# The last four attention tiles in a written-out order, and where a weight transpose stands in the SyncE queue (cross-attention and quantized feed-forward, one core)

## The chip, the cores and the metric

One Trainium2 chip, one core, one launch of the whole program. The time is the device time of that launch in microseconds. Three runs of the kernel before give a median of 570.4 us (570.27 to 570.66).

## What is computed

Eight sequences of 512 rows of 512 numbers, each with its own context of 77 rows of 384. A layer norm, cross-attention with 8 heads of 64, an output product with a bias and a residual; then a second layer norm and a gated feed-forward of width 1408 whose activations and weights are fake-quantized, the activations by a scale over the whole tensor, and a second residual.

```python
def xattn(x, context):                      # x already normed
    q, k, v = heads(x @ Wq), heads(context @ Wk), heads(context @ Wv)
    a = softmax(einsum('bhsd,bhld->bhsl', q, k) * 64 ** -0.5)
    return merge(einsum('bhsl,bhld->bhsd', a, v)) @ Wo + bo
x = x + xattn(layernorm(x), ctx)
xq = act_quant(layernorm(x), clip_x)        # scale: max |.| of all 8*512*512 numbers / 127
h = silu(xq @ w_quant(w_gate).T) * (xq @ w_quant(w_up).T)
x = x + act_quant(h, clip_down) @ w_quant(w_down).T
```

## The kernel before, in words

The 4096 rows are 32 row tiles of 128; a batch b is the four tiles 4b to 4b+3. The order on every engine is written out by hand: each helper appends one instruction (or one group) to the list of its engine with the tokens (semaphore, value) that it waits for, and each engine runs its list in order. A DMA is issued by SyncE ("SPq"), in the order of its list as well; both transposing DMAs are in that list (L39).

`attend(s)` (L647), called for s = 0 to 31 (L844), is one step of a software pipeline. For tile s it turns the normed probabilities (`PT`, L425: five transposes into the bank pair `PTP`; `PT_high` on ScalarE and `PT_low` on VectorE split them into a high and a low half in `pts`). For tile s+1 it makes the scores (`S`, L375, into the bank pair `SP`), takes the maximum and subtracts it (`soft_max`, `soft_sub`, VectorE), exponentiates (ScalarE), sums and inverts (VectorE) and multiplies by the inverse (`soft_norm`, GpSimd). `S(n)` waits for `soft_sub(n-1)`, since both use `SP`. For tile s-5 it makes the output product (`wo`, L487: 12 matmuls into the single bank `WOP`), adds the residual (`residual`, L517, VectorE, whose result `x1` is stored) and the statistics of the second norm (`second_stats`, `second_aggr`, `second_scale`). For s-6 it norms (`normed`, L541, ScalarE; the result `n2` is stored to `n_rows` in HBM), for s-7 it takes the largest magnitude (`largest`, L548). Four buffers of `x1` and of `n2` exist (RR = 4): `normed(n)` waits for the landing of the store of `n2` of tile n-4.

At t = 0 of a batch the product with the values of the batch before is made (`PV_rest`, `PV`, L448 to L481) in the two banks of `QO` and the two of `SP`; its results are split into `os`, which `wo` reads. Up to s = 23 there are also projections of queries (`q_chunk`) into `QO`; from s = 24 on there are none, and `QO` is used by `PV` alone.

The weights of the feed-forward are quantized on the way (`w_load` to `w_integer`) and their integers stored. Two transposing DMAs bring them back: `wgu` (gate and up, L858) and `wd` (down, L926). The diagonal of the four scales of `w_down` rows (L854, VectorE) is spread to all partitions by four matmuls with ones into the bank `MI` (`spread_scale`, L834) and copied to `sdb`.

After the loop come `wo(27)`, `PV` of batch 7, and for the tiles 28 to 31 product, residual, statistics, norm and largest (L878). With that the barrier is reached: `whole_scale(0)` (L904) reduces the 32 columns of largest magnitudes to one number on all partitions, with small matmuls between (`keep_clock`, L896). The first four tiles of `n2` are loaded back into `n2b` (L887), multiplied by the scale (`quant_y`), rounded (`quant_top`, `quant_low`), turned (`turn`) and fed to the feed-forward's matmuls (`ffn`, L968). `quant_top` writes over memory of the first half, and so waits for `flown` (L925): the landing of all stores of `x1` and `n2` of the tiles 28 to 31.

The SyncE list around this place: the twelve loads of `vbd` for batch 7, then the transpose `wgu`, then stores of `x1` and `n2` as they come, four loads of `n2b` after the stores of tile 30's `x1`, the last stores, four more loads, the transpose `wd`.

## Time and profile before

| | |
|---|---|
| median of three runs | 570.4 us |
| the profiled execution | 570.46 us, span of its instructions 568.6 us |
| start to the last tiles (0 to 271.2 us) | TensorE busy 258.2 us |
| last tiles of attention (271.2 to 294.3) | TensorE busy 18.9 of 23.1 us, VectorE 21.35 |
| PV of batch 7 and the last four products (294.3 to 309.4) | TensorE busy 15.1 of 15.1 us |
| barrier (309.4 to 320.7) | TensorE busy 9.75 of 11.3 us |
| gate and up products (320.7 to 484.6) | TensorE busy 163.84 of 163.9 us |
| down products and the end (484.6 to 568.6) | TensorE busy 77.2 of 84.0 us |

The profiled execution's own time is 0.06 us above the median, and 1.9 us above its span. A row of the trace gives start, length, engine, line of the code, operation, and what it writes and reads; in brackets stands the idle time of the engine before it and who ended it. Starts are counted from the first instruction. Short operations of one engine overlap by some 0.1 us, so that lengths may add up to more than the time between starts.

### The profile page before, as it was taken

The numbers are of one execution on the slowest core, as the hardware profiler recorded it, in microseconds if no ns is written. First come the engines' busy times: TensorE is split into PE (matmuls) and PEld (weight loads), VectorE is DVE, ScalarE is ACT, GpSimd is POOL, SyncE is SP. The second block draws the span as 40 slices with busy tenths as digits, with TensorE's granted clock in tenths as the row PEclk, the third lists the DMA queues.
The fourth block names the chain that finished last, engine by engine and source line by source line (L and its number), as shares of the span: only waits on it lengthen the run. The fifth ranks groups of instructions, "written<-read, shape, count | busy, mean of one in ns | idle before, by whom it ended". The sixth has DMA issues, their size and how long they took to land.

```text
span 568.6 us, 8277 instructions
## 1 busy us (share of the span) xinstructions
PE 543.0 (95%) x2811; PEld 360.7 (63%) x2811; DVE 471.8 (83%) x874; ACT 310.4 (55%) x436; POOL 233.9 (41%) x352
## 2 busy tenths in 40 slices
PE   4999889999999999999899899999999999899997
PEld 2978678787888878787668544444444446443443
DVE  2747888989989888998987689889888988879883
ACT  3743546556464755544342666666666643999300
POOL 3576758679595968856342000000000000054442
PEclk9999999999999999999999999999999999999999
DMA  8708365756657573633295917541020010299887
GB/s 309 256 38 277 107 196 171 249 168 207 214 178 231 194 249 115 215 118 126 73 317 189 261 62 278 203 148 47 29 75 1 0 38 1 100 339 217 118 107 119
DMA packets 67779, 90.16 MB, mean 159 GB/s; under 512 B 32049, under 2 KB 34865, under 8 KB 67481
## 3 DMA queue, kind: packets, MB, share of 16 engines
q1 hardware_dynamic: 63413, 81.77, 44.6%
q0 software_dynamic: 4320, 7.87, 9.3%
q8 instruction: 22, 0.36, 0.3%
q14 instruction: 20, 0.16, 0.1%
q10 hardware_dynamic: 4, 0.00, 0.0%
HBM read 47.51 MB, written 37.78 MB: 150 GB/s over the span
## 4 chain that ended last, share of the span: by engine, by line
PE 50%; issue 34%; DVE 8%; DMA 5%; ACT 1%; POOL 1%; SPq 0%; POOLq 0%; DVEq 0%
PE QO L194 6%; PE QO L196 6%; PE QO L195 6%; PE SP L382 5%; PE WOP L495 4%; PE WOP L493 4%; PE WOP L494 4%; DMA out<-n2b 2%; PE PTP L1082 2%; PE PTP L430 2%; PE QO L1082 2%; PE SP L1082 2%; DMA wkr<-in_xattn_Wk 2%; PE MI L1082 1%; PE WOP L1082 1%
## 5 line engine op out<-in xcount | busy, mean ns | idle before, releaser
L45 POOL DMA_DIRECT2D out<-n2b x30 | 30.2, 1039 | 219.1 <-DVE n2b L1093 219.1
L977 PE MATMUL QO<-nT,wgu 128*128 128x512 bf16 x352 | 90.3, 379 | 0.6 <-ACT nT L221 0.6
L977 PE MATMUL SP<-nT,wgu 128*128 128x512 bf16 x352 | 90.3, 379 | 0.0
L983 ACT ACTIVATE sil<-QO,fsc 128x512 f32<-128x512 f32 x88 | 60.5, 687 | 50.7 <-PE QO L977 45.4
L987 DVE SCALAR_TENSOR_TENSOR h<-SP,fsc,sil 128x512 f32<-128x512 f32 x88 | 65.9, 749 | 14.9 <-PE SP L977 14.7
L422 POOL TENSOR_TENSOR PN<-P,rs 128x512 f32<-128x512 f32 x64 | 44.2, 712 | 57.8 <-DVE rs L414 57.8
L405 ACT ACTIVATE P<-P,r 128x616 f32<-128x616 f32 x32 | 26.0, 812 | 69.5 <-DVE P L401 69.5
L990 DVE TENSOR_REDUCE hmx<-h 128x1 f32<-128x512 f32 x88 | 60.4, 686 | 3.0
L977 PEld LDWEIGHTS SP<-nT,wgu 128*128 128x128 bf16 x352 | 34.4, 98 | 41.5
L977 PEld LDWEIGHTS QO<-nT,wgu 128*128 128x128 bf16 x352 | 33.2, 98 | 35.4 <-ACT nT L221 0.7
L194 PE MATMUL QO<-xTs,wqs 128*128 128x512 f32 x128 | 52.0, 407 | 1.8 <-DVE xTs L225 1.3
L196 PE MATMUL QO<-xTs,wqs 128*128 128x512 f32 x128 | 50.1, 391 | 0.0
L195 PE MATMUL QO<-xTs,wqs 128*128 128x512 f32 x128 | 49.9, 390 | 0.0
L1051 ACT ACTIVATE h<-h,magic,g 128x1536 f32<-128x1536 f32 (+2 forms) x38 | 47.8, 1354 | 3.7 <-DVE g L222 3.7
L493 PE MATMUL WOP<-wos,os 128*128 128x512 f32 x116 | 47.6, 411 | 0.2 <-DVE x L519 0.2
L495 PE MATMUL WOP<-wos,os 128*128 128x512 f32 x116 | 45.9, 395 | 0.0
L494 PE MATMUL WOP<-wos,os 128*128 128x512 f32 x116 | 45.8, 395 | 0.0
L382 PE MATMUL SP<-kst,qs 128*128 128x154 f32 x256 | 39.5, 296 | 5.0 <-DVE P L401 2.9
L514 POOL TENSOR_TENSOR xn<-xn,bob 128x512 f32<-128x512 f32 x32 | 41.2, 1291 | 0.0
L590 ACT ACTIVATE wraw<-wraw,magic,wiv 128x512 f32<-128x512 f32 (+1 forms) x26 | 24.1, 928 | 30.3 <-DVE wiv L583 30.3
L382 PEld LDWEIGHTS SP<-kst,qs 128*128 128x128 f32 x256 | 35.5, 190 | 7.3 <-DVE P L401 3.8
L543 ACT ACTIVATE n<-x,mr,r 128x512 f32<-128x512 f32 x32 | 25.8, 807 | 20.0 <-POOL mr L537 20.0
(169 smaller groups left out, 1162.9 us busy)
## 6 DMA issues: line engine op xcount, KB each, us to landing
xTr<-in_xT SPq DMA_DIRECT2D x8, 1024.0 KB, 8.0
xn<-in_x SPq DMA_DIRECT2D x32, 256.0 KB, 3.8
out<-x SPq DMA_DIRECT2D x32, 256.0 KB, 2.9
n_rows<-n SPq DMA_DIRECT2D x32, 256.0 KB, 2.6
n2b<-n_rows SPq DMA_DIRECT2D x32, 256.0 KB, 4.2
out<-n2b POOLq DMA_DIRECT2D x30, 256.0 KB, 4.4
h_spill<-h SPq DMA_DIRECT2D x2, 2816.0 KB, 9.3
h<-h_spill SPq DMA_DIRECT2D x6, 768.0 KB, 7.8
```

The costliest lines, as they stand in the source:

```text
L194: e.matmul(ps, lh, rh, start=(i == 0), stop=False)
L195: e.matmul(ps, lh, rl, start=False, stop=False)
L196: m = e.matmul(ps, ll, rh, start=False, stop=(i == n - 1))
L382: m = e.matmul(o, qs[:, b % 2, j, w], kst[:, b, j, :], start=(j % 2 == 0), stop=True, skip_group_check=True)
L493: e.matmul(wo_bank(n), os_[:, 0, j, w], wos[:, 0, j, :], start=(j == 0), stop=False)
L494: e.matmul(wo_bank(n), os_[:, 0, j, w], wos[:, 1, j, :], start=False, stop=False)
L495: return e.matmul(wo_bank(n), os_[:, 1, j, w], wos[:, 0, j, :], start=False, stop=(j == 3))
L977: m = e.matmul(ps, wv_[:, k, col:col + 128], nT[:, b % 2, k, :], start=(k == 0), stop=(k == 3))
L983: t_sil[n] = add("act", lambda e: e.activation(sil[:, n % SR, :], gp, ACT.Silu, scale=fsc[:, ic:ic + 1]), [t_g[n], t_fs, t_h.get(n - SR)] ...
L987: t_h[n] = add("dve", lambda e: e.scalar_tensor_tensor(out=hv, in0=up, scalar=fsc[:, 11 + ic:12 + ic], in1=sil[:, n % SR, :], op0=ALU.mult ...
L990: t_hm[n] = add("dve", lambda e: e.tensor_reduce(hmx[:, n:n + 1], hv, AX.X, ALU.max, apply_absolute_value=True), [t_h[n]], "hmx")
L1051: a = add("act", lambda e: e.activation(hv, hv, ACT.Identity, bias=magic[:, :], scale=g2[:, 1, 1:2]), [t_g2] + ([t_back[b, p]] if b < 2 el ...
```

## The change

1. The loop over `attend` ends at s = 27. The work of the steps 28 to 31, and of the lines after the loop up to `PV(7, 3)`, is a written-out list, `last_batch`. In it `S(30)` and `PT(30)` use the bank pair `QO`, so that `S(30)` waits for the low halves of `PV(6, 0)` and `PV(6, 1)` and not for `soft_sub(29)`, and `PT(31)` doesn't wait for `PT_low(30)`. `second(26)`, `second(27)` and `normed(26)` stand at its end, behind `PV(7, 3)`.
2. The output products alternate between `WOP` and `MI` (those of the tiles 30 and 31 use `PTP` and `SP`), and wait for the residual of tile n-2 where they waited for n-1.
3. The diagonal of weight scales moves from VectorE to ScalarE, behind `normed(26)`; its four matmuls and the copy (now ScalarE) stand behind the last output product. `keep_clock` issues 8 instead of 20 in front of the first barrier.
4. The call of the transpose `wgu` stood in the loop at s = 28; it now stands behind `last_batch()`. `largest` of the tiles 24 to 29 is called in pairs in the last loop.

```diff
+        def S_bank(n):
+            return QO if n == 30 else SP
...
         def S(n):
+            if n == 30:
+                free = [t_oss[6, 0], t_oss[6, 1]]
+            else:
+                free = [t_sub[29] if n == 31 else t_sub.get(n - 1)]
...
+        def PT_bank(n):
+            return QO if n == 30 else PTP
...
         def PT(n):
+            free = t_sub[30] if n == 30 else t_pl[29] if n == 31 else t_pl.get(n - 1)
...
         def wo_bank(n):
-            return {28: PTP[:, 0:512], 29: SP[:, 0:512], 31: SP[:, 512:1024]}.get(n, WOP[:, :])
+            return {30: PTP[:, 0:512], 31: SP[:, 0:512]}.get(n, (WOP, MI)[n % 2][:, :])
...
         def wo(n):
-            free = t_x1.get(n - 1) if n < 28 else (t_pl[31], t_oss[7, 2], t_x1[27], t_oss[7, 3])[n - 28]
+            free = {30: t_pl[31], 31: t_oss[7, 2]}[n] if n >= 30 else t_x1.get(n - 2)
...
+        def last_batch():
+            def second(n):
+                second_stats(n); second_aggr(n); second_scale(n)
+            normed(22); first_stats(31); first_aggr(31); first_scale(31)
+            wo(23); residual(23); PV_rest(6); second(23)
+            for j in (2, 3, 0, 1):
+                PV(6, j)
+            PT(28); S(29); S(30); PT_high(28)
+            soft_max(29); soft_sub(29); load_vb(7); soft_exp(29)
+            soft_max(30); soft_sub(30); PT_low(28); soft_exp(30)
+            normed(23); soft_sum(29); soft_rec(29); soft_norm(29)
+            wo(24); S(31)
+            soft_sum(30); soft_rec(30); soft_norm(30)
+            soft_max(31); soft_sub(31); soft_exp(31)
+            wo(25); residual(24); PT(29); PT_high(29)
+            soft_sum(31); soft_rec(31); soft_norm(31); PT_low(29)
+            wo(26); residual(25); second(24); largest(21); first_bias(31)
+            PT(30); PT_high(30); PT(31); PT_high(31)
+            normed(24); PT_low(30); PT_low(31)
+            state["free"][0] = state["free"][1] = (t_pl[30],)
+            wo(27); residual(26); PV_rest(7); second(25); residual(27); largest(22)
+            for j in range(4):
+                PV(7, j)
+                if j == 0:
+                    normed(25)
+            second(26); second(27); largest(23); normed(26)
...
-        for s in range(32):
+        for s in range(28):
             attend(s)
-            if s == 28:
-                for r in range(4):
-                    dgt = wraw[:, 0, r * 128:r * 128 + 128]
-                    t = add("dve", lambda e, r=r, dgt=dgt: e.tensor_scalar_mul(
-                        dgt, identF[:, :], wsc[:, 22 + r:23 + r]),
-                        [t_idF, t_wsc[25], t_wb[24], t_wb[25]], "dg")
-                t_dgs.append(t)
-                t_wgu = c.dma_turn(wgu[:, :].rearrange("p (k n) -> p k n", k=4), wgud,
-                                   [t_qh[7, 3], t_ws[24], t_ws[25]], "ld_wgu")
...
+        last_batch()
+        t_wgu = c.dma_turn(wgu[:, :].rearrange("p (k n) -> p k n", k=4), wgud,
+                           [t_qh[7, 3], t_ws[24], t_ws[25]], "ld_wgu")
+        gone = [t_S[31], t_q[7]]
+        for r in range(4):
+            dgt = wraw[:, 0, r * 128:r * 128 + 128]
+            t_dg = add("act", lambda e, r=r, dgt=dgt: e.activation(dgt, identF[:, :], ACT.Identity,
+                                                                   scale=wsc[:, 22 + r:23 + r]),
+                       [t_idF, t_wsc[25], t_wb[24], t_wb[25]], "dg")
         for n in range(28, NT):
             wo(n)
             normed(n - 1)
             residual(n)
...
-            if n > 28:
-                largest(n - 2)
+            if n < 31:
+                largest(2 * n - 32)
+                largest(2 * n - 31)
             if n == 30:
-                load_n2(0, gone[:2] + [t_n2s[tt] for tt in range(4)])
+                load_n2(0, gone + [t_n2s[tt] for tt in range(4)])
...
+        def spread_scale(e):
+            for r in range(4):
+                m = e.matmul(QO[:, 512 + r * 128:640 + r * 128], ones[:, :], wraw[:, 0, r * 128:r * 128 + 128],
+                             start=True, stop=True)
+            return m
+        t = add("pe", spread_scale, [t_dg, t_oss[7, 1]], "sd_mm")
+        t_sdb = copy("act", sdb[:, :], QO[:, 512:1024], [t], "sdb")
...
-            keep_clock(20 if which == 0 else 8)
+            keep_clock(8)
```

The lines of `last_batch` are joined here by semicolons; each call is a line of its own in the file.

The SyncE queue before, from the `vbd` loads of batch 7 on (`n_rows<-n` and `out<-x` are stores of `n2` and `x1`, `n2b<-n_rows` the loads behind the barrier):

```order
L37 DMA vbd<-v_halves 13x2x64 x8
L41 DMA_TRANSPOSE wgu<-wgu_ints 128x4x2816
L37 DMA out<-x 128x512
L37 DMA n_rows<-n 128x512
L37 DMA out<-x 128x512
L37 DMA n_rows<-n 128x512
L37 DMA out<-x 128x512
L37 DMA n_rows<-n 128x512 x2
L37 DMA out<-x 128x512
```

The same queue now, from just ahead of the transpose:

```order
L37 DMA out<-x 128x512 x2
L37 DMA n_rows<-n 128x512 x2
L41 DMA_TRANSPOSE wgu<-wgu_ints 128x4x2816
L37 DMA n_rows<-n 128x512
L37 DMA out<-x 128x512
L37 DMA n_rows<-n 128x512
L37 DMA out<-x 128x512
L37 DMA n_rows<-n 128x512
L37 DMA out<-x 128x512
L37 DMA n2b<-n_rows 128x512 x4
L37 DMA n_rows<-n 128x512
L37 DMA out<-x 128x512
```

The transpose has moved behind the stores of `x1` of tile 27 and of `n2` of tile 26. Behind it now stand, in this order, the stores `n2` 27, `x1` 28, `n2` 28, `x1` 29, `n2` 29, `x1` 30, the four loads of `n2b`, and the stores `n2` 30, `x1` 31 and (the row after these) `n2` 31: thirteen transfers, the last store being the thirteenth.

TensorE before, from `PT(28)` on (the x8 are `S(29)` and `S(30)`):

```order
L430 MATMUL PTP<-identF,PN 128x128 x5
L382 MATMUL SP<-kst,qs 128x154 x8
L493 MATMUL WOP<-wos,os 128x512
L494 MATMUL WOP<-wos,os 128x512
L495 MATMUL WOP<-wos,os 128x512
```

And now:

```order
L443 MATMUL PTP<-identF,PN 128x128 x5
L390 MATMUL SP<-kst,qs 128x154 x4
L390 MATMUL QO<-kst,qs 128x154 x4
L508 MATMUL WOP<-wos,os 128x512
L509 MATMUL WOP<-wos,os 128x512
L510 MATMUL WOP<-wos,os 128x512
```

The order of these is the same, but `S(30)` has its own banks. Further on, the matmuls of the scales (L838) no longer stand between `wo(24)` and `PT(29)`.

## Rows read from the trace of the kernel before

**Rows 1.** Busy time by stage: us, then busy us by engine, TensorE's granted clock, DMA share, GB/s.

```profile
core 0: us, PE busy (x) PEld busy (x) DVE busy (x) ACT busy (x) POOL busy (x), PEclk, DMA share, GB/s
271.20:294.30 23.10, 18.90 (x101) 14.82 (x99) 21.35 (x37) 7.75 (x12) 9.60 (x20) 1.00 0.69 158
294.30:309.40 15.10, 15.10 (x73) 11.80 (x73) 11.27 (x20) 5.54 (x8) 4.00 (x12) 1.00 0.57 214
309.40:320.70 11.30, 9.75 (x89) 8.98 (x88) 8.00 (x23) 6.31 (x9) 1.27 (x4) 1.00 1.01 291
320.70:484.60 163.90, 163.84 (x863) 80.54 (x864) 144.13 (x243) 98.78 (x147) 0.00 (x0) 1.00 0.26 85
```

**Rows 2.** Timeline of TensorE, last tiles: start us, us, what [idle before <-releaser].

```profile
271.18 0.71 PE L430 MATMUL PTP<-identF,PN 128*128 128x128 f32 x5
271.73 1.27 PE L382 MATMUL SP<-kst,qs 128*128 128x154 f32 x8
274.94 1.32 PE L382 MATMUL SP<-kst,qs 128*128 128x154 f32 x8 [1.95 <-DVE P L401]
276.00 0.50 PE L493 MATMUL WOP<-wos,os 128*128 128x512 f32 x1
...
279.63 1.16 PE L838 MATMUL MI<-wraw,ones 128*128 128x128 f32 x8 [0.57 <-DVE wraw L854]
280.63 0.71 PE L430 MATMUL PTP<-identF,PN 128*128 128x128 f32 x5
...
290.83 0.76 PE L430 MATMUL PTP<-identF,PN 128*128 128x128 f32 x5 [1.23 <-POOL PN L422]
...
294.33 0.51 PE L463 MATMUL QO<-pts,vbd 32*128 32x512 f32 x2
...
295.23 0.50 PE L471 MATMUL QO<-pts,vbd 128*128 128x512 f32 x1
...
309.40 4.62 PE L900 MATMUL WOP<-ones 128*128 128x128 f32 x40
```

**Rows 3.** Timeline of VectorE and ScalarE in the barrier, and TensorE's first product behind it.

```profile
310.32 0.69 DVE L525 BATCH_NORM_STATS2 bn<-x 128x6 f32<-128x512 f32 x1
...
313.39 0.69 DVE L549 TENSOR_REDUCE amx<-n 128x1 f32<-128x512 f32 x1 [0.99 <-ACT n L543]
315.86 0.16 DVE L222 COPY g<-MI 128x2 f32<-128x2 f32 x1 [0.50 <-PE MI L917]
316.92 0.76 DVE L945 TENSOR_SCALAR qb<-n2b 128x512 bf16<-128x512 f32 x2
...
312.54 0.81 ACT L543 ACTIVATE n<-x,mr,r 128x512 f32<-128x512 f32 x1 [1.99 <-POOL mr L537]
313.37 1.28 ACT L894 ACT_TABLE_LOAD   x1
...
320.69 1.02 PE L977 MATMUL QO<-nT,wgu 128*128 128x512 bf16 x4 [0.56 <-ACT nT L221]
```

**Rows 4.** Timeline of the SyncE queue (SPq): start and length of the issue.

```profile
281.54 10.75 SPq L41 DMA_TRANSPOSE wgu<-wgu_ints  x1
292.34 0.57 SPq L37 DMA_DIRECT2D out<-x  x1
296.77 1.31 SPq L37 DMA_DIRECT2D out<-x  x1
...
311.13 0.43 SPq L37 DMA_DIRECT2D out<-x  x1
313.38 0.32 SPq L37 DMA_DIRECT2D n_rows<-n  x1
```

**Rows 5.** DMA issues at 281.54, 292.34, 296.77, 311.13, 313.38: KB, us to landing.

```profile
wgu<-wgu_ints SPq DMA_TRANSPOSE x1, 13.6
out<-x SPq DMA_DIRECT2D x1, 256.0 KB, 3.3
out<-x SPq DMA_DIRECT2D x1, 256.0 KB, 4.4
out<-x SPq DMA_DIRECT2D x1, 256.0 KB, 4.3
n_rows<-n SPq DMA_DIRECT2D x1, 256.0 KB, 2.7
```

**Rows 6.** Timeline of VectorE, the same stretch.

```profile
271.48 1.28 DVE L478 TENSOR_TENSOR os<-QO,os 128x512 fp32r<-128x512 f32 x2
276.71 2.86 DVE L854 TENSOR_SCALAR wraw<-identF,wsc 128x128 f32<-128x128 f32 x4
299.46 0.68 DVE L478 TENSOR_TENSOR os<-SP,os 128x512 fp32r<-128x512 f32 x1
```

**Rows 7.** Busy time by stretch, behind the transpose and in the barrier (columns as in rows 1).

```profile
284.00:292.00 8.00, 6.62 (x33) 4.88 (x32) 7.89 (x15) 2.47 (x4) 4.50 (x10) 1.00 1.26 284
309.00:316.00 7.00, 6.67 (x56) 6.26 (x55) 4.38 (x12) 3.11 (x4) 1.61 (x5) 1.00 1.02 338
```

**Rows 8.** TensorE's first instruction of the program.

```profile
6.37 6.42 PE L269 MATMUL WOP<-wqr,ones 128*128 128x512 f32 x8 [6.37 <-DMA wqr<-in_xattn_Wq]
```

More of the change, by code:

```diff
@@ L832, in load_n2 @@
                 t_nl[b, tt] = dma("sp", n2b[:, b % 2, tt, :], n2d[4 * b + tt], waits, f"ld_n2b{b % 2}{tt}")
-        def spread_scale():
-            def fn(e):
-                for r in range(4):
-                    m = e.matmul(MI[:, r * 128:r * 128 + 128], ones[:, :],
-                                 wraw[:, 0, r * 128:r * 128 + 128], start=True, stop=True)
-                return m
-            t = add("pe", fn, t_dgs, "sd_mm")
-            t_dgs.append(copy("dve", sdb[:, :], MI[:, :], [t], "sdb"))
@@ L844, in block_kernel @@
-        for s in range(32):
+        def last_batch():
+            def second(n):
+                second_stats(n)
+                second_aggr(n)
+                second_scale(n)
+            normed(22)
+            first_stats(31)
+            first_aggr(31)
+            first_scale(31)
+            wo(23)
+            residual(23)
+            PV_rest(6)
+            second(23)
+            for j in (2, 3, 0, 1):
+                PV(6, j)
+            PT(28)
+            S(29)
+            S(30)
+            PT_high(28)
+            soft_max(29)
+            soft_sub(29)
+            load_vb(7)
+            soft_exp(29)
+            soft_max(30)
+            soft_sub(30)
+            PT_low(28)
+            soft_exp(30)
+            normed(23)
+            soft_sum(29)
+            soft_rec(29)
+            soft_norm(29)
+            wo(24)
+            S(31)
+            soft_sum(30)
+            soft_rec(30)
+            soft_norm(30)
+            soft_max(31)
+            soft_sub(31)
+            soft_exp(31)
+            wo(25)
+            residual(24)
+            PT(29)
+            PT_high(29)
+            soft_sum(31)
+            soft_rec(31)
+            soft_norm(31)
+            PT_low(29)
+            wo(26)
+            residual(25)
+            second(24)
+            largest(21)
+            first_bias(31)
+            PT(30)
+            PT_high(30)
+            PT(31)
+            PT_high(31)
+            normed(24)
+            PT_low(30)
+            PT_low(31)
+            state["free"][0] = state["free"][1] = (t_pl[30],)
+            wo(27)
+            residual(26)
+            PV_rest(7)
+            second(25)
+            residual(27)
+            largest(22)
+            for j in range(4):
+                PV(7, j)
+                if j == 0:
+                    normed(25)
+            second(26)
+            second(27)
+            largest(23)
+            normed(26)
@@ L891, in block_kernel @@
         largest(31)
[L892 removed]
+        load_n2(1, gone + [t_n2s[4 + tt] for tt in range(4)])
+        def spread_scale(e):
[5 more added lines that the diff above has]
+        t_sdb = copy("act", sdb[:, :], QO[:, 512:1024], [t], "sdb")
         add("act", lambda e: e.activation(warm[:, :], sge[:, :], ACT.Silu), [t_sge], "warm")
```

67 lines of the change are left out of this document (21 added, 46 removed).

## The prediction

> **What bounds the kernel now.** I read the busy time by stage first. Behind the barrier TensorE is busy for 163.84 of 163.9 us, so what starts it late is paid in full, and what starts it early is won in full. The attention's last tiles are the one stage here in which it waits: 18.9 busy of 23.1 us, while VectorE has 21.35 [rows 1]. The timeline of TensorE shows where: 1.95 us ahead of `S(30)`, which waits for the subtraction of tile 29; 0.57 ahead of the matmuls of the weight scales, which wait for VectorE's four multiplications; 1.23 ahead of `PT(31)` [rows 2]. Then comes the barrier, a chain: norm of tile 31, its largest magnitude, the scale at 316.02, `quant_top` at 316.92, the first gate product at 320.69 [rows 3].
>
> Beside it I read the SyncE queue, because the change moves one thing in it. The transpose `wgu` holds the queue for 10.75 us, 281.54 to 292.29, and the store behind it is issued at 292.34 [rows 4]. Nobody needed those stores at once. It lands 13.6 us after its issue begins, and the store issued at 292.34 lands 3.3 us later, at 295.6, so 14.1 us behind the transpose's start; the one issued at 313.38 took 2.7 [rows 5]. So the transfers keep their order: what stands behind the transpose lands behind it.
>
> **The change on TensorE.** `PT(28)` starts at 271.18 and `S(29)` at 271.73; one group of scores takes 1.0 us in the stream (1.06 from 274.94 to 276.00) [rows 2]. `S(30)` in `QO` waits for the low halves there, which end at 271.48 + 1.28 = 272.76 [rows 6]; it ends at 273.8. An output product costs 2.83 us (from 295.23 to 309.40 there are 12 + 48 matmuls: 0.236 each, times 12), 2.9 with the change of operand ahead of it; a `PT` 0.55 (271.18 to 271.73) [rows 2]. Up to batch 7's `PV_rest` there now stand four products (11.6), `S(31)` (1.0) and three `PT` (1.65), and no scale matmuls: 273.8 + 14.25 = 288.05, against 294.33, **6.3 us earlier**. Can VectorE feed that? Of its 21.35 us the four scale multiplications (2.86 [rows 6]) and the copy of the scales (about 0.65, as long as other copies of 512 columns) go away, and three of four `largest` (0.6 each in the stream) wait until later: 16.0 us of work for 16.9 us. It fits, with little to spare. Alternating the banks of the output products takes a wait away that was hardly there; it counts as nothing, since all of this turns out to be hidden.
>
> **The change on the queue.** The transpose now stands behind the store of `n2` of tile 26, and that norm has been put behind all of `PV(7)`. Before, the last low half of batch 7 ended 5.8 us after `PV_rest` began (299.46 + 0.68 = 300.14, less 294.33) [rows 2, 6]; one `largest` stood between, so now 5.55: 293.6. From statistics to norm it is 2.2 us (310.32 to 312.54), the norm takes 0.8 [rows 3], the issue of its store 0.35 [rows 4]: the **transpose is issued at 296.95**, 15.4 us later than before. The queue is held until 307.7. The first store behind it, `n2` of tile 27, lands at 296.95 + 14.1 = 311.05.
>
> Two things wait for what stands behind. First, `normed(31)` reuses tile 27's buffer. TensorE is done with its last product 6.3 us earlier, at 303.1, and the norm could start 3.1 us later (309.40 to 312.54 [rows 2, 3]), at 306.2. It starts at 311.1 instead and ends at 311.9. That is still 1.4 us earlier than before (313.35), so the scale comes at 314.6. ScalarE then has the copy of the scales (0.65), a table load (1.28) and the small warm-up (0.2): done at 314.1, hidden.
>
> Second, `quant_top` waits for all stores of tiles 28 to 31, the last of which is the thirteenth transfer behind the transpose. Each moves 256 KB. The pace I bound from two sides: the last two stores before landed at 311.13 + 4.3 = 315.4 and 313.38 + 2.7 = 316.1, 0.65 us apart; the eight behind the transpose landed from 295.6 to 296.77 + 4.4 = 301.2, 0.79 us apart [rows 4, 5]. The stage's 338 GB/s [rows 7] would make it 0.775. I take 0.72, in the middle, since part of each long gap was waiting for an issue and the new queue is full. Twelve steps: 311.05 + 8.65 = 319.7. The four loads of `n2b` are the 7th to 10th, in by 317.6, and do not decide. **`quant_top` starts at 319.75 and not at 316.92: 2.8 us later.** From there to the first gate product it is the same 3.8 us [rows 3], and behind it nothing changes.
>
> The other edits, the scale matmuls behind the last product (1.0 us, in front of a wait of 8 us), `dg` on ScalarE (which waits for GpSimd there) and 8 in place of 20 in `keep_clock`, cost nothing by themselves; the cover is the wait for the queue. If the queue were free, the scale matmuls would be covered by the norm of tile 31 alone (3.1 us), still enough.
>
> Sum against the profiled execution: 570.46 + 2.8 = **573.3 us**, 2.9 above the median of 570.4. With paces of 0.65 and 0.79 and half a microsecond either way for the transpose's issue it is 571.9 to 574.6. A difference under 0.2%, 1.1 us, can hardly be told from none.
>
> By rows the transpose moved 284 GB/s while it filled the engines [rows 7]. The Trainium skill, "DMA: Bandwidth & Descriptors", section "Latency and other measured facts", gives a transposing DMA with a non-contiguous middle dimension 261 GB/s. By that the transfer would take about 0.9 us more and the sum would be some 3.7 us; the measured 13.6 us decides.
>
> **Rivals.**
> *The clock falls.* TensorE would have 1.0 us of scale matmuls and 16 short ones behind 303.1, then nothing from about 305.1 to 312.7, against an almost busy barrier before (9.75 of 11.3) [rows 1]. The trace has no such pause at full clock. The nearest row is the start of the program: eight passes of 512 columns in 6.42 us, 0.80 each [rows 8], where forty of 128 columns took 4.62, thus 0.46 for four times as many columns [rows 2]; that fits the 1.2 GHz level. If the gate products start at that level and stay for those 6.4 us, they lose half of it, 3.2 us: 576.5. Against it: the small matmuls of the barrier would run from 312.7 on, at half speed for longer, some 4 to 6 us of work, and could bring the clock back before 323.5. Chance 0.22, at 574.5 to 576.5. (The Trainium skill, "TensorE: Matmul & The Clock Gate", Part 1, says that an idle TensorE falls to half its clock and that sustained work releases it; by that rule the fall in the pause is certain, and only what the products lose is open.)
> *The queue drains in time.* If the thirteen transfers need 0.45 us each, the last lands at 316.5 and the result is 570 to 571.5. No row shows such a pace. Chance 0.11.
> *The queue does not hold: faster.* If the 10.75 us are no property of the transpose but came from the `vbd` loads in front of it, SyncE would issue the stores on time, and if they passed the transpose's packets, `normed(31)` would start at 306.2 and the whole barrier 6.3 us earlier: 570.46 - 6.3 = 564.2. The point where it decides is the landing of the last store: before 316.1 the change wins. For it: an issue of this length is shown once. Against it: the landings were in the queue's order, and the engines were full meanwhile (284 GB/s). Chance 0.12.
>
> **How the numbers follow.** Forecast 0.55; clock 0.22; drains in time 0.11; faster 0.12. Forecast and clock are slower by over 0.2%, 0.77; same 0.11; faster 0.12. The likeliest case's own range is 571.9 to 574.6. For 8 in 10 I go down to 570.9, into the second rival, and up to 576.4, nearly the whole of the first.
>
> **What would show it.** Right: `wgu` issued near 297 and the queue held to 307.7; TensorE's last output product ending near 303; an idle stretch of some 7 us on ScalarE ahead of the last norm and on TensorE ahead of the largest's transpose; `quant_top` near 319.7, ended by a DMA landing; 163.9 us of gate and up products as before. Wrong: the last norm before 308 (the queue did not hold), `PV_rest` of batch 7 later than 290 (VectorE did not keep up), gate products of more than 1.02 us for four (the clock), or a transpose of another length.

## The result, and the profile after

The changed kernel takes **574.9 us** (median; 573.3 to 575.2), the kernel before 570.4 (570.3 to 570.7): a ratio of 1.0073, with a 95% interval of 1.0054 to 1.0092. The change makes the kernel slower. (The ratio is estimated over the executions and comes to 4.2 us; the two medians lie 4.5 apart.) The profiled execution is the quickest of the four: 573.29 us, with a span of 571.5, against 570.46 and 568.6 before.

One thing has to be taken off before the two traces are laid side by side. All times of the trace after are 1.1 us earlier from 204 us on: before, VectorE waited 1.24 us there for the load of a tile of `x`, and now it did not. The only part of the change that reaches that place is the second bank of the output products, and in experiment 4 the wait stands as before although the bank is there. The same wait (0.73 to 1.32 us) stands in three of the eleven profiles of the changed kernel and its variants, and in all three of the kernel before and its variants, in which `PT(28)` starts between 270.39 and 271.18; in the eleven it is 269.71 to 270.96. So a wait of this kind comes and goes with the landing of a load. Whether the change makes it rarer is not settled by so few profiles, and what follows is counted from `PT(28)`: 271.18 before, 270.07 now.

Busy time by stage, after (to be set against [rows 1] and [rows 7]; same columns):

```profile
270.10:287.10 17.00, 17.00 (x97) 14.13 (x95) 15.66 (x26) 7.17 (x11) 7.95 (x15) 1.00 0.28 90
287.10:302.20 15.10, 15.10 (x74) 11.82 (x74) 13.50 (x27) 7.09 (x13) 5.26 (x17) 1.00 0.57 156
302.20:311.30 9.10, 2.79 (x25) 2.60 (x23) 3.71 (x8) 2.56 (x4) 1.82 (x5) 0.84 1.20 327
311.30:322.80 11.50, 7.00 (x47) 6.24 (x49) 4.58 (x16) 4.34 (x7) 0.00 (x0) 0.80 1.01 301
322.80:326.50 3.70, 3.69 (x12) 1.42 (x12) 0.71 (x1) 1.39 (x2) 0.00 (x0) 0.65 1.28 255
```

The last tiles now take 17.0 us in place of 23.1, and TensorE does not wait once in them. Everything won there is lost in the third and fourth line: the barrier, 11.3 us before with 9.75 busy, is 20.6 us long with 9.8 busy. And the column of the granted clock, 1.00 in every stage before, is under 1 in the last three lines. Cut finer, the clock is 0.50 from 308.4 to 315.1, 1.00 from 315.2 to 321.9 and 0.50 again from 322.0 to 325.3.

Timeline of TensorE, after (against [rows 2] and the last row of [rows 3]):

```profile
270.07 0.71 PE L443 MATMUL PTP<-identF,PN 128*128 128x128 f32 x5
...
271.98 1.29 PE L390 MATMUL QO<-kst,qs 128*128 128x154 f32 x8
...
287.08 0.50 PE L478 MATMUL QO<-pts,vbd 32*128 32x512 f32 x2
...
303.05 1.95 PE L967 MATMUL WOP<-ones 128*128 128x128 f32 x16
311.34 0.37 PE L975 MATMUL MI<-identF,gcol 128*1 128x128 f32 x1 [6.34 <-DVE gcol L974]
311.51 1.91 PE L967 MATMUL WOP<-ones 128*128 128x128 f32 x8
...
319.83 0.62 PE L1026 MATMUL PTP<-identB,qb 128*128 128x128 bf16 x8 [2.88 <-DVE qb L1018]
...
322.81 1.49 PE L1044 MATMUL QO<-nT,wgu 128*128 128x512 bf16 x3 [0.94 <-ACT nT L221]
324.09 1.66 PE L1044 MATMUL SP<-nT,wgu 128*128 128x512 bf16 x4
325.59 1.03 PE L1044 MATMUL QO<-nT,wgu 128*128 128x512 bf16 x4
```

Three waits of the kernel before are gone (1.95, 0.57, 1.23), and two new ones stand in the barrier (6.34, 2.88). Behind the first, eight small matmuls of 128 columns take 1.91 us, twice the 1.05 that they take in the barrier of the second experiment. The first gate products run at half speed too. Of the first group one record is missing (three matmuls, and 0.94 idle where the other groups have 0.56), so the products begin at about 322.4; the first eight end their turn at 325.59, 3.2 us later, where at full clock eight take 1.73 (twice the 0.86 between groups of four). That is 1.4 us lost to the clock. From `PT(28)` to the products it is 49.5 us before and 52.4 now (322.4 less 270.07), 2.85 more; with the clock's 1.4 that makes **4.3 us**, close to the 4.5 between the medians. The change run once more (experiment 3) gives 4.1 us in the same way, where its medians give 4.2.

The SyncE queue, after (against [rows 4]), and then the landings of its issues at 296.10, 306.82 and 313.65 (against [rows 5]):

```profile
296.10 10.67 SPq L41 DMA_TRANSPOSE wgu<-wgu_ints  x1
306.82 0.57 SPq L37 DMA_DIRECT2D n_rows<-n  x1
...
313.65 0.49 SPq L37 DMA_DIRECT2D n_rows<-n  x1
```

```profile
wgu<-wgu_ints SPq DMA_TRANSPOSE x1, 12.7
n_rows<-n SPq DMA_DIRECT2D x1, 256.0 KB, 2.6
n_rows<-n SPq DMA_DIRECT2D x1, 256.0 KB, 5.0
```

VectorE and ScalarE in the barrier, after (against [rows 3]):

```profile
309.53 0.81 ACT L558 ACTIVATE n<-x,mr,r 128x512 f32<-128x512 f32 x1 [5.57 <-DMA n_rows<-n]
310.38 0.69 DVE L564 TENSOR_REDUCE amx<-n 128x1 f32<-128x512 f32 x1 [5.27 <-ACT n L558]
...
313.97 0.16 DVE L222 COPY g<-MI 128x2 f32<-128x2 f32 x1 [1.52 <-PE MI L984]
...
318.81 0.76 DVE L1012 TENSOR_SCALAR qb<-n2b 128x512 bf16<-128x512 f32 x2 [2.23 <-DMA n_rows<-n]
```

Read together: the transpose holds the queue from 296.10 to 306.77. The store of tile 27's `n2` is issued then and lands at 309.4; at 309.53 ScalarE starts the last norm, which had waited 5.57 us for it. The last store is issued at 313.65 and lands at 318.7; at 318.81 `quant_top` starts, which had waited 2.23 us for that. Both brackets name the same queue.

### The profile page after: what moved, and what is told of

It reads as the page before. It is cut to its first block, busy times and chain, and to the rows that moved or that the text cites. A ratio compares the mean times of both kernels' runs of the same rounds, so it can differ in the third digit from the quotient of the medians.

```text
span 571.5 us, 8211 instructions
## 1 busy us (share of the span) xinstructions
PE 539.8 (94%) x2763; PEld 360.0 (63%) x2787; DVE 468.3 (82%) x869; ACT 311.7 (55%) x441; POOL 234.5 (41%) x352
## 4 chain that ended last, share of the span: by engine, by line
PE 84%; DVE 4%; ACT 4%; SPq 3%; DMA 2%; issue 1%; POOL 0%; DVEq 0%
PE SP L1044 13%; PE QO L1044 13%; PE QO L194 6%; PE QO L196 6%; PE QO L195 6%; PE SP L390 5%; PE PTP L1149 3%; PE PTP L443 3%; PE QO L1149 2%; PE SP L1149 2%; PE WOP L508 2%; PE WOP L510 2%; PE WOP L509 2%; PE MI L510 2%; PE MI L508 2%; PE MI L509 2%
## 5 line engine op out<-in xcount | busy, mean ns | idle before, releaser
L390 PE MATMUL SP<-kst,qs 128*128 128x154 f32 x248 | 38.0, 295 | 2.3 <-DVE os L493 1.5
L558 ACT ACTIVATE n<-x,mr,r 128x512 f32<-128x512 f32 x32 | 25.8, 807 | 20.7 <-POOL mr L552 15.1
L225 POOL TENSOR_TENSOR xTs<-xTr,xTs 128x512 fp32r<-128x512 f32 x21 | 27.5, 1335 | 9.1 <-ACT xTs L221 9.0
L1121 DVE TENSOR_SCALAR wgu<-h 128x1536 bf16<-128x1536 f32 (+2 forms) x39 | 29.4, 755 | 2.0 <-ACT h L1118 1.3
L194 PEld LDWEIGHTS QO<-xTs,wqs 128*128 128x128 f32 x128 | 24.0, 188 | 7.4 <-issue 1.6
```

Of the source, the lines that this page charges most:

```text
L194: e.matmul(ps, lh, rh, start=(i == 0), stop=False)
L390: m = e.matmul(o, qs[:, b % 2, j, w], kst[:, b, j, :], start=(j % 2 == 0), stop=True, skip_group_check=True)
```

## The experiments

All were run beside the kernel before, which had medians of 570.04, 569.84 and 569.89 us in the three groups (single executions 568.9 to 571.9, so these runs scatter more than the four above). Experiments 1, 2, 4 and the first kernel of 5 are of the first group, 3 and 6 to 8 of the second, the second kernel of 5 and 9 to 11 of the third. Times below are medians.

**1. The transpose early, the rest of the change kept.** If the queue is what costs, the change without its fourth part should win.

```diff
 def last_batch():
 ...
             load_vb(7)
+            turned_in["wgu"] = c.dma_turn(wgu..., wgud, [t_qh[7, 3], t_ws[24], t_ws[25]], "ld_wgu")
             soft_exp(29)
 ...
         last_batch()
-        t_wgu = c.dma_turn(wgu..., wgud, [t_qh[7, 3], t_ws[24], t_ws[25]], "ld_wgu")
+        t_wgu = turned_in["wgu"]
```

> The changed kernel with one move: the transpose wgu is issued right behind the vbd loads of batch 7, where it stood before the change. Theory (its place in the SyncE queue ate the gain): the queue is free when the last stores come, the last norm starts some 3 us behind TensorE's last product, and the 6.3 us of the attention's end arrive: 564.2 us, 563.5 to 565.5. Rival 1 (the barrier as rebuilt gives the gain back by itself, or the clock falls there anyway): 568 or more. Rival 2 (the transpose now delays the store of tile 23's norm and of tile 24's x1, whose buffers are wanted again near 295 us): 565.5 to 568, with a wait for a DMA landing ahead of the residual of tile 28 or the norm of tile 27.

It takes 566.04 us (ratio 0.9939, 0.9919 to 0.9960): 8 to 9 us less than the change, and 4.0 less than before. Queue, VectorE and TensorE:

```profile
280.34 10.57 SPq L41 DMA_TRANSPOSE wgu<-wgu_ints  x1
...
312.09 0.16 DVE L222 COPY g<-MI 128x2 f32<-128x2 f32 x1 [1.53 <-PE MI L987]
...
317.98 1.02 PE L1047 MATMUL QO<-nT,wgu 128*128 128x512 bf16 x4 [0.56 <-ACT nT L221]
```

The executions lie between 564.4 and 570.1, and the profiled one, 567.2, is in their slower half. So the sign of the result hangs on one call. The 564.2 that was expected is missed; 566.0 is what the second rival had, a store behind the early transpose that holds up a later tile. TensorE is 6.1 us earlier here (its last output product ends 32.1 us behind `PT(28)`, before 38.2), and 4.0 of that arrive. Four things in the profile take some of it: the last residual starts at 304.71, 1.8 us later than in the change (302.91); TensorE paused for 4.64 us, and by the half clock behind that pause the way to the scale is 1.1 us longer (308.49 to 312.09, 3.60, in place of 2.47 [rows 3]); the last store lands at 313.03 and `quant_top` starts at 313.15; and the twenty small matmuls behind the scale, at half clock too, end so late that the first turn starts at 315.38, 2.2 us behind `quant_top`, where it was 1.2 (316.92 to 318.09). Experiments 6 to 8 take them up.

**2. The transpose late, nothing else.** The kernel before, with that one call moved behind `largest(26)`.

```diff
-                t_wgu = c.dma_turn(wgu..., wgud, [t_qh[7, 3], t_ws[24], t_ws[25]], "ld_wgu")
 ...
         largest(26)
+        t_wgu = c.dma_turn(wgu..., wgud, [t_qh[7, 3], t_ws[24], t_ws[25]], "ld_wgu")
         for n in range(28, NT):
```

> The kernel before with only the transpose wgu moved behind PV of batch 7, that is behind the stores of x1 of tile 27 and of n2 of tile 26; all other work in its old order, 20 groups in the first keep_clock. Theory: issued near 295.9 us; in the changed kernel the last of the thirteen transfers landed 22.6 us behind the transpose's issue, so here at 318.5; quant_top starts at 318.6 in place of 316.9: 1.7 us slower, 572.1 us (571.5 to 572.8), with the granted clock at 1.0 throughout. Rival (the place of the transpose is harmless as long as TensorE isn't early): 570.4, within 0.5.

574.95 us (ratio 1.0084, 1.0065 to 1.0103): 4.9 us slower than before, where 1.7 were expected. The place of the transpose alone costs as much as the whole change. Queue, TensorE and VectorE:

```profile
296.63 11.05 SPq L41 DMA_TRANSPOSE wgu<-wgu_ints  x1
...
314.14 1.05 PE L900 MATMUL WOP<-ones 128*128 128x128 f32 x8
...
319.34 0.76 DVE L945 TENSOR_SCALAR qb<-n2b 128x512 bf16<-128x512 f32 x2 [2.40 <-DMA n_rows<-n]
320.36 0.62 PE L959 MATMUL PTP<-identB,qb 128*128 128x128 bf16 x8 [2.42 <-DVE qb L951]
...
322.97 1.87 PE L977 MATMUL QO<-nT,wgu 128*128 128x512 bf16 x4 [0.56 <-ACT nT L221]
324.63 1.83 PE L977 MATMUL SP<-nT,wgu 128*128 128x512 bf16 x4
326.30 1.03 PE L977 MATMUL QO<-nT,wgu 128*128 128x512 bf16 x4
```

The mechanism holds, `quant_top` waits for the store, but it is later than expected: 319.34 where 318.6 was forecast and 316.92 stood before; counted from `PT(28)`, here at 270.39, it is 3.2 us later than before and not 1.7. The transpose was issued 26.2 us behind `PT(28)` where 24.7 had been reckoned; from its issue to the last landing it was 22.6 us, as forecast. The forecast for the clock fails. In the barrier it was 1.00 up to the small matmuls, TensorE paused for 2.4 us only, and yet the first eight products took 3.33 us (322.97 to 326.30) in place of 1.73. From `PT(28)` the products start 3.1 us later than before, and with the 1.6 of the clock that is 4.7 of the 4.9 us in the medians. So a fall of the clock at the products does not need the long pause of the change. Nor is it the only fall here: the clock was at 0.50 from 275.1 to 278.4 as well, behind the old wait of 1.95 us ahead of `S(30)`. It fell at this place in experiment 4 too, while the profile of the kernel before, with the same wait, shows 1.00 there.

**3. The change once more, unedited**, as the reference for the second group.

> The changed kernel once more, as the neighbour of the next three on the same chip. 573.3 to 576, median near 575, with the granted clock under 1.0 in the gate products; a median at 573.3 would say that the fall of the clock there was chance.

574.0 us (ratio 1.0064, 1.0041 to 1.0088), with the same trace: the same two pauses of TensorE (6.47 and 2.79 us), the last store in at 318.5, half clock behind both. The five executions, by the mean granted clock of each: 0.993 with 571.7 us, 0.991 with 572.8, 0.988 with 574.0, 575.0 and 575.2. The kernel before, in the same group, has 0.997 to 0.999. The longer executions are those with more time at the low clock. The quickest, 571.7, has less of it than the profiled one (0.993 against 0.991) and is 1.1 us quicker.

**4. Two product banks in the kernel before.** This isolates the second part of the change up to tile 23, and tests whether the 1.1 us at 204 us belong to it.

```diff
+            if n < 24:
+                return (WOP, MI)[n % 2][:, :]
 ...
-            free = t_x1.get(n - 1) if n < 28 else ...
+            free = t_x1.get(n - 2) if n < 24 else t_x1.get(n - 1) if n < 28 else ...
```

> The kernel before with only the output products of the tiles 0 to 23 alternating between WOP and MI and waiting for the residual of tile n-2. In the changed kernel everything from 204 us on stood 0.9 to 1.1 us earlier than before, where before VectorE waited 1.24 us for the load of an x tile. Theory A (chance or a knock-on of DMA times, not the banks): 570.4 within 0.4. Theory B (the second bank takes the knock-on of such waits away): 569.4, 0.9 to 1.1 us faster, TensorE's last tiles starting at 270.1 in place of 271.2.

569.6 us (ratio 0.9992, 0.9984 to 1.0001): no difference. VectorE still waits for the load, for as long as before:

```profile
203.62 0.69 DVE L502 BATCH_NORM_STATS2 bn<-xn 128x6 f32<-128x512 f32 x1 [1.47 <-DMA xn<-in_x]
```

So the second bank does not remove that wait.

**5. The clock kept up by more small matmuls** (two kernels). What does the low clock cost in the median? The change, with the pauses filled: in the first 38 and 24 pairs of small matmuls in place of 8 and 10, in the second 36 and 29.

```diff
-            keep_clock(8)
+            keep_clock(38 if which == 0 else 8)      # second kernel: 36
 ...
-            keep_clock(10)
+            keep_clock(24 if which == 0 else 10)     # second kernel: 29
```

> The changed kernel with 38 in place of 8 groups in front of the barrier's first transpose and 24 in place of 10 behind the scale, so that TensorE is kept busy through both pauses; nothing else is moved and no product waits longer. Theory (the part above 573.3 is the clock: granted 0.5 twice, and how far the second fall reaches into the gate products differs by execution): granted clock 0.999 or more, the first four groups of gate and up products at 0.86 us each, 572.2 us (571.6 to 572.9), and the executions agree within 0.5 us. Rival (executions differ by how fast the queue drains): still 573.3 to 575.2 and scattered.

575.79 us (ratio 1.0097, 1.0082 to 1.0112) where 572.2 was expected: not faster. The profiled execution is its slowest (577.08). TensorE, first kernel:

```profile
321.32 0.62 PE L1026 MATMUL PTP<-identB,qb 128*128 128x128 bf16 x8 [2.90 <-DVE qb L1018]
...
324.13 1.86 PE L1044 MATMUL QO<-nT,wgu 128*128 128x512 bf16 x4 [0.56 <-ACT nT L221]
325.80 1.91 PE L1044 MATMUL SP<-nT,wgu 128*128 128x512 bf16 x4
327.50 1.78 PE L1044 MATMUL QO<-nT,wgu 128*128 128x512 bf16 x4
```

The long pause was gone and the scale came 1.1 us sooner (312.90 in place of 313.97), but a pause of 2.90 us remained ahead of the transposes of `qb`, and twelve products ran at half clock. The last store landed at 320.2, 1.5 us later than in the change.

> The changed kernel with 36 in place of 8 groups in the first keep_clock and 29 in place of 10 in the one behind the scale. With 24 there, TensorE still paused 2.9 us ahead of the transposes and the clock fell at 322.2 us, so nothing was learned of its price. 29 groups last 6.7 us from 313.0 and end where the transposes of the quantized tiles have begun, near 319.7. Theory (the clock costs about 1.1 us in the profiled executions of the changed kernel and more in its median, 574.0 to 574.9): no fall ahead of the gate products, their groups 0.86 us each from the first, 572.3 us (571.5 to 573.0). Rival (the clock falls whatever fills the pauses, or the median's excess is the queue's): 574 or more.

574.41 us (ratio 1.0083, 1.0055 to 1.0111); 572.3 was expected, the rival had 574 or more. TensorE, second kernel:

```profile
312.81 6.74 PE L967 MATMUL WOP<-ones 128*128 128x128 f32 x58
320.75 0.62 PE L1026 MATMUL PTP<-identB,qb 128*128 128x128 bf16 x8 [1.20 <-DVE qb L1018]
...
323.94 1.48 PE L1044 MATMUL QO<-nT,wgu 128*128 128x512 bf16 x3 [0.94 <-ACT nT L221]
325.22 1.12 PE L1044 MATMUL SP<-nT,wgu 128*128 128x512 bf16 x4
```

Only 1.20 us of pause was left, and the clock still fell, at 322.0, between the short transposes and the products. It cost less (about 0.9 us of the eight products), and the queue ended 0.9 us later (319.6 against 318.7), which ate it. Neither kernel beats the change, and neither keeps the clock at the products in its profile. But two of the four executions of the second kernel have a mean clock of 0.999, so they lost next to nothing to it, and took 573.96 and 574.23 us; the two at 0.996, the profiled one among them, took 574.60 and 576.41. Even with the clock kept, then, this kernel is 4.1 to 4.3 us behind the kernel before (569.89). The queue is the likely reason, in the profile 0.9 us later still than in the change; but the executions at 0.999 were not profiled, so this is argued. **What the clock costs the change in the median was not isolated.** What is shown is its 1.4 us in the profiled execution, and that filling the pauses in this way brings nothing while the stores set the end. Whether the busier TensorE and the slower queue have to do with each other is open; it is one profile each.

**6. Early transpose, clock kept.** Experiment 1 with `keep_clock(20)` in front of the barrier.

```diff
-            keep_clock(8)
+            keep_clock(20 if which == 0 else 8)
```

> The early transpose (e1_turn_early), with 20 in place of 8 groups in the first keep_clock. In that run the clock fell at 307.4 us in a pause of 4.6 us and the chain from the largest to the scale took 3.0 us in place of 1.9; but its quant_top at 313.15 also had to wait for the last store, landed at 313.03. Theory (the stores decide there): the scale comes 1 us earlier and the time stays within 0.4 of that kernel's 566.0. Rival (the clock decides): 1.0 us or more faster, 565.0 or less.

565.7 us (ratio 0.9926, 0.9899 to 0.9953), not distinguishable from experiment 1, as expected. The clock was 1.00 throughout, also behind a pause of 1.99 us ahead of the largest's transpose. VectorE:

```profile
297.88 0.69 DVE L534 TENSOR_TENSOR x<-WOP,xn 128x512 f32<-128x512 f32 x1 [2.12 <-DMA out<-x]
...
313.89 0.76 DVE L1015 TENSOR_SCALAR qb<-n2b 128x512 bf16<-128x512 f32 x2 [0.47 <-DMA n_rows<-n]
```

Both waits end with a store. The first is the one of experiment 1's rival, and it stands there too (1.88 us): the residual of tile 28 writes the buffer of tile 24, whose `x1` store stood two places behind the transpose. The early transpose of experiment 1 was one store too early.

**7. The transpose behind the store of tile 24.** It moves down by two stores (`n2` of 23, `x1` of 24).

```diff
             residual(24)
+            turned_in["wgu"] = c.dma_turn(wgu..., wgud, [t_qh[7, 3], t_ws[24], t_ws[25]], "ld_wgu")
             PT(29)
```

> The early transpose moved behind two stores, n2 of tile 23 and x1 of tile 24, that stood right behind it; 8 groups in keep_clock. With the early transpose x1 of tile 24 landed at 296.4 us, while the residual of tile 28, which reuses its buffer, could have run at 294.9; the last residual ended 1.8 us later than in the changed kernel. Theory: with the two stores ahead that wait is gone, the last residual starts near 303.0 in place of 304.7, the last store lands 1.5 us earlier, 564.5 us (563.8 to 565.3). Rival (another transfer's landing, tile 25's x1 or tile 24's n2, takes its place): 566.0 within 0.4, with such a wait in the trace.

565.27 us (ratio 0.9923, 0.9904 to 0.9942). That wait is gone, the last residual starts at 303.34 (304.71 in experiment 1), and the last store lands at 310.56, 2.5 us sooner than there. The first gate product comes at 316.05 (317.98 there). The median moves by 0.8 us, less than the trace. What is left is TensorE's own: behind a pause of 2.67 us the clock fell at 309.6, and the small matmuls behind the scale took 4.13 us in place of 2.50:

```profile
309.48 4.13 PE L970 MATMUL WOP<-ones 128*128 128x128 f32 x20
313.45 0.61 PE L1029 MATMUL PTP<-identB,qb 128*128 128x128 bf16 x8
```

**8. All of it together.** Experiment 7, `keep_clock(18)`, and the first four loads of `n2b` called one step earlier.

```diff
-            if n == 30:
+            if n == 29:
                 load_n2(0, gone + [t_n2s[tt] for tt in range(4)])
 ...
-            keep_clock(8)
+            keep_clock(18 if which == 0 else 8)
```

> That kernel with 18 groups in keep_clock, and the four loads of n2b called at tile 29 and not at tile 30, two stores earlier in the queue. The loads are 4 x 0.65 us of the queue in front of the last stores. Theory (once the transpose is out of the way the last stores are the bound, and the loads in front of them count): the last store lands near 309.5 us, quant_top near 310.3, 562 us (561 to 563.3). Rival (the chain largest, scale, quantization is the bound now): as e6_behind_x24 within 0.5.

**564.25 us** (ratio 0.9899, 0.9880 to 0.9919): 5.6 us faster than the kernel before and about 10 faster than the change. Queue, TensorE and VectorE:

```profile
280.88 10.64 SPq L41 DMA_TRANSPOSE wgu<-wgu_ints  x1
...
303.18 4.18 PE L970 MATMUL WOP<-ones 128*128 128x128 f32 x36
307.81 0.27 PE L978 MATMUL MI<-identF,gcol 128*1 128x128 f32 x1 [0.44 <-DVE gcol L977]
...
309.21 2.50 PE L970 MATMUL WOP<-ones 128*128 128x128 f32 x20
...
310.38 0.76 DVE L1015 TENSOR_SCALAR qb<-n2b 128x512 bf16<-128x512 f32 x2
...
314.14 1.02 PE L1047 MATMUL QO<-nT,wgu 128*128 128x512 bf16 x4 [0.56 <-ACT nT L221]
```

The pauses of TensorE are gone (0.44 in place of 6.34), `quant_top` waits for no store, and the first gate product starts at 314.14, 43.9 us behind `PT(28)` (270.25) where it was 49.5: the 5.6 us of the medians. The norm of the last tile, the scale and the turns are a chain of computation again. Of the two edits on top of experiment 7 only `keep_clock` shows in the trace. The last store lands 1.2 us sooner by the earlier loads (38.9 us behind `PT(28)`, 40.1 there), but `quant_top` starts 40.1 and 40.2 us behind it, since the scale decides. The first turn comes 1.2 us behind `quant_top` and 2.8 in experiment 7, where the half-speed matmuls stand in front of it. That is 1.6 of the 1.7 us by which the traces differ; the medians differ by 1.0. So the expectation of 562 failed in its mechanism: the last stores were no longer what decides. Its rival, as experiment 7 within 0.5, failed as well, since it left the clock out. The 562 had also been worked out from absolute times, the head start at 204 us with them, which is no gain to count on (this profile starts 0.9 us ahead of before, and its execution is at 563.51).

The last three kernels undo one part of the reordering each, against experiment 8.

**9. Without the query banks.** `S(30)` and `PT(30)` go back to the banks of the other tiles, in the old order.

```diff
-            return QO if n == 30 else SP
+            return SP
 ...
-                free = [t_oss[6, 0], t_oss[6, 1]]
+            free = [t_sub.get(n - 1)]
 ...
-            return QO if n == 30 else PTP
+            return PTP
 ...
             S(29)
-            S(30)
             PT_high(28)
 ...
             soft_sub(29)
+            S(30)
```

> The fastest version so far (e7_all_three, 564.3) with S(30) and PT(30) back in SP and PTP: S(30) waits for the subtraction of tile 29, PT(31) for the low half of tile 30; the order on every engine is unchanged. Theory: S(30) starts 1.75 us later (273.75 in place of 272.0) and PT(31) again about 1.2 us later, TensorE's waits there come back, 567.2 us (565.8 to 568.2). Rival (VectorE bounds these tiles and takes the waits in): within 0.5 of 564.3.

567.86 us (ratio 0.9961, 0.9943 to 0.9978), 3.6 us more than experiment 8. Waits of TensorE in the last tiles:

```profile
273.44 1.32 PE L387 MATMUL SP<-kst,qs 128*128 128x154 f32 x8 [1.73 <-DVE P L407]
...
287.04 0.74 PE L440 MATMUL PTP<-identF,PN 128*128 128x128 f32 x5 [1.74 <-DVE pts L225]
```

The two waits add up to 3.5 us, against 3.6 in the medians. What TensorE waits for here is paid in full once the queue does not cover it.

**10. One product bank.** The output products up to tile 29 use `WOP` alone, each behind the residual of the one before.

```diff
-            return {30: PTP[:, 0:512], 31: SP[:, 0:512]}.get(n, (WOP, MI)[n % 2][:, :])
+            return {30: PTP[:, 0:512], 31: SP[:, 0:512]}.get(n, WOP[:, :])
 ...
-            free = ... t_x1.get(n - 2)
+            free = ... t_x1.get(n - 1)
 ...
-            wo(25)
             residual(24)
+            wo(25)                 # the same for 26 and 27
```

> The same fastest version with all output products up to tile 29 in WOP alone, each waiting for the residual of the tile before it, as the kernel before had it; orders unchanged on every engine. In the written-out order the products stand one residual earlier than before, so they should now wait: wo(25) from 276.9 to 280.0, wo(26) to near 285, wo(27) to near 291. Theory: some 7 us slower, 571.3 us (569.5 to 573). Rival (the second bank does nothing, as for the tiles 0 to 23): within 0.5 of 564.3.

576.51 us (ratio 1.0104, 1.0069 to 1.0140), 12.3 us more than experiment 8, where 7 were expected. Waits of TensorE:

```profile
280.09 0.50 PE L508 MATMUL WOP<-wos,os 128*128 128x512 f32 x1 [2.90 <-DVE x L534]
...
285.96 0.79 PE L508 MATMUL WOP<-wos,os 128*128 128x512 f32 x1 [2.25 <-DVE x L534]
...
294.06 0.50 PE L508 MATMUL WOP<-wos,os 128*128 128x512 f32 x1 [2.44 <-DVE x L534]
```

With the fourth (1.62, at 305.49) that is 9.2 us of waits, and the clock fell once behind the second (0.50 from 286.0 to 289.3). The one execution with a mean clock of 1.00 took 573.25, 9.0 more than experiment 8, about the waits alone; the other four, at 0.991 to 0.997, took 574.48 to 578.09. The two banks, worth nothing in the order of the kernel before (experiment 4), carry the new one.

**11. The weight scales back on VectorE**, behind `soft_rec(29)`.

```diff
             soft_rec(29)
+            for r in range(4):
+                dgt = wraw[:, 0, r * 128:r * 128 + 128]
+                turned_in["dg"] = add("dve", ... tensor_scalar_mul(dgt, identF, wsc[:, 22 + r:23 + r]) ...)
             soft_norm(29)
 ...
-            t_dg = add("act", ... activation(dgt, identF, ACT.Identity, scale=wsc[:, 22 + r:23 + r]) ...)
+        t_dg = turned_in["dg"]
```

> The same fastest version with the four multiplications of the scale diagonal back on VectorE, behind the inverse of tile 29; the matmuls and the copy stay behind the last product. Theory: VectorE has 15.7 us of work in the 17.0 us up to PV of batch 7, and 2.9 more don't fit; the low half of tile 31 comes 1.3 to 2.3 us later than TensorE wants it, 566.0 us (565.3 to 566.8). Rival (absorbed): within 0.5 of 564.3.

565.6 us (ratio 0.9921, 0.9897 to 0.9945), 1.35 us more than experiment 8, as expected; the two sets of executions, 564.84 to 566.19 and 563.51 to 564.99, just overlap. Wait of TensorE:

```profile
282.56 0.51 PE L508 MATMUL WOP<-wos,os 128*128 128x512 f32 x1 [1.34 <-DVE x L534]
```

The four multiplications took 1.82 us here (2.86 before [rows 6]). In a stretch in which VectorE has 15.7 of 17.0 us of work, 1.82 more push it behind TensorE.

## Why the prediction was right

The forecast was 573.3 us with a range of 570.9 to 576.4; the median is 574.9, inside and 1.6 above, and the profiled execution 573.29. But it is inside only by the part of the range that was added for the clock: the likeliest case had 571.9 to 574.6 of its own, and the rival of the clock 574.5 to 576.5. The queue was forecast rightly, and the clock came on top. Step by step, in times from `PT(28)`:

| step | forecast | measured |
|---|---|---|
| `S(30)` starts | 1.6 | 1.91 |
| `PV_rest` of batch 7 | 16.9 | 17.01 |
| last output product ends | 31.9 | 32.1 |
| transpose issued | 25.8 | 26.03 |
| first store behind it lands | 39.9 | 39.4 |
| last norm starts | 39.9 | 39.46 |
| last store lands | 48.5 | 48.6 |
| `quant_top` starts | 48.6 | 48.74 |
| first gate product | 52.3 | 52.4 |

- *TensorE and VectorE.* VectorE had 15.66 us of work for the 17.00 (forecast 16.0 for 16.9), and TensorE waited for nothing. Experiments 9 to 11 say which parts do that: 3.6, 12.3 and 1.35 us, each measured with the others in place. "It counts as nothing", said of the two banks, is true of the old order only. With one bank in the changed kernel, TensorE would by experiment 10 (9.2 us of waits) end its products near 311.4 and not 302.2, and the last norm could not start at 309.53. That is an estimate; it was not run with the late transpose.
- *The queue.* It was held for 10.67 us (10.75 before), and what stood behind the transpose landed behind it. The first store landed 13.4 us behind the transpose's start where 14.1 were forecast, and the twelve that follow took 0.77 us each (from 309.4 to 318.7) where 0.72 were taken. The two errors, 0.7 less and 0.6 more, cancel: that part of the hit is luck. One small term has no row behind it: 5.8 us less one `largest` (0.6) is 5.2 and not 5.55; measured from `PV_rest` to the end of the last low half it was 5.6.
- *Hidden work.* The scale matmuls, the copy and the table load on ScalarE cost nothing. In the cover of the queue lay one thing more: at half clock the way from the last largest magnitude to the scale took 3.59 us (310.38 to 313.97) in place of 2.47 (313.39 to 315.86 [rows 3]).
- *The sum.* From `PT(28)` to the first gate product it is 2.85 us more than before (forecast 2.8). The profiled executions differ by 2.8 us too, and that is luck: 1.1 less at 204 us, 2.85 more, 1.4 more at the gate products, together 3.1 (the spans differ by 2.9).
- *The rivals.* "The queue does not hold" fell: 10.55 to 11.18 us of issue in every kernel, wherever the transpose stood and also with stores ahead of it, and in the trace after the store behind the transpose lands after it (309.4 against 308.8). "Drains in time" fell with a pace of 0.77. "**The clock falls**" came true beside the forecast, not in its place. The step that failed is the one that let the small matmuls bring the clock back for good: they did bring it back (1.00 from 315.1 to 322.0), and it fell again behind the pause of 2.88 us, ahead of the products. The forecast had looked at one pause and there were two. Its own sign of being wrong, gate products of more than 1.02 us for four, came (1.66 for the second group). The price is 1.4 us in the profiled execution, not the 3.2 of the rival, and near the 1.6 us by which the median lies above the forecast. That the other executions lost this at the same place is argued, not shown: they have a mean clock of 0.985 to 0.988 where the profiled one has 0.991, so they ran longer still at the low level, and where is not recorded.
- *The pages.* The Trainium skill, "DMA: Bandwidth & Descriptors", section "Latency and other measured facts", gives 261 GB/s for a transposing DMA with a non-contiguous middle dimension, by which the transfer would have been an estimated 0.9 us longer than before. The trace does not agree: the queue moved 290 GB/s from 300 to 306 us, and from issue to landing the transpose took 12.7 us, less than the 13.6 before. The Trainium skill, "TensorE: Matmul & The Clock Gate", Part 1, says that an idle TensorE falls to half its clock; behind the pause of 6.34 us the trace agrees (eight matmuls in 1.91 us in place of 1.05).

## What to carry to other kernels

A DMA whose issue holds its queue for 10.7 us is to be costed by what stands behind it in that queue and by when somebody needs its landing, not by its own data: moved by 15 us it turned a gain of 4.0 us (experiment 1; 4.6 at the better place of experiment 7) into a loss of 4.2 to 4.5. Look at both kinds of waiters, those for the last landing (`quant_top`) and those for a buffer that a store still reads (the last norm, the residual of tile 28); the best of the three places tried was right behind the last store that somebody would soon wait for. Not run: the same transpose issued from another engine's queue, which would be the direct way around. And where an engine is made faster, read on to the next stage for what it now waits for, and look there for every pause of TensorE, not the longest alone. Small matmuls that are to keep the clock up stand in TensorE's list like any others: if the clock falls nevertheless, they take 4.13 us in place of 2.50 and hold up what stands behind them (experiment 7).

## What the runs showed that had not been expected

- The clock fell at the first gate products behind a pause of 2.4 us (experiment 2) and of 1.20 us (experiment 5, second kernel), each followed by groups of eight 128-column bf16 transposes with 0.56 us between them. The length of the pause alone does not tell: it stayed at 1.00 behind 1.99 us in experiment 6 and behind 1.73 and 1.74 in experiment 9, and behind 1.95 us ahead of `S(30)` it fell in the profiles of experiments 2 and 4 but not in that of the kernel before.
- A store two places behind a long transfer can hold up VectorE four tiles later through its buffer (2.12 us, experiment 6). The diff of experiment 1 does not show it, but its expectation had it as a rival.
- From one profile to the next of the changed kernel and its variants, `PT(28)` starts up to 1.3 us apart, in part by the landing of one load (waits of 0.73 to 1.32 us), as much as some of the effects that were looked for. A common mark in both traces (here `PT(28)`) takes it out: by it the trace gives 4.3 and -5.6 us where the medians give 4.5 and -5.6.
